# Delta-rule attention on one core: VectorE's value and key taps and substitution rows re-ordered, GpSimd's roots ahead of its weighting with two added waits, and the identity block loaded by DMA

## The chip, the cores and the metric

The kernel runs on 1 core of one Trainium2 chip. The metric is the device time of one execution in microseconds (us). Times of single instructions come from one profiled execution. Engines are named as the profile names them: PE (TensorE, with its weight loads as PEld), DVE (VectorE), ACT (ScalarE), POOL (GpSimd), SP (SyncE); SPq and ACTq are the DMA issues of SP and ScalarE.

## The reference, cut to what matters

Two layers follow each other, each with a residual and a layer norm: a gated delta-rule attention over 2 sequences of 2048 tokens (16 heads of 64), then a mixture of 64 experts. The change touches the attention alone.

```python
q = _causal_dwconv(x @ Wq.T, cq_w, cq_b)      # 4 taps in time, per channel; the same for k and v
k = _causal_dwconv(x @ Wk.T, ck_w, ck_b)
v = _causal_dwconv(x @ Wv.T, cv_w, cv_b)
g, beta = log_sigmoid(x @ Wg.T), sigmoid(x @ Wb.T)
k = k / clip(norm(k), 1e-12)
q = q * Kd ** (-0.5)
def step(S, inp):                              # over the 2048 tokens
    q_t, k_t, v_t, g_t, b_t = inp
    delta = k_t v_t^T - k_t (S k_t)^T
    S = exp(g_t) * S + b_t * delta
    o_t = S q_t
```

The kernel computes the recurrence in chunks of 64 tokens. Within a chunk that takes the inverse of a unit triangular 64x64 matrix; its 16x16 diagonal blocks are inverted by substitution, row by row, beginning from the identity, and the rest by products.

## The kernel before

**Work and slots.** The attention (`delta_phase`) has 64 macros: a macro m is one pair of heads over 256 tokens (4 chunks) of both sequences. All engines walk the same 71 slots t, each with a list of its own written out by hand in the code. In slot t the macro m = t is projected and convolved, the macro `before` = t-1 gets its lengths, decays and masked products, the macro `mi` = t-5 its inverse, and the state recurrence (the chain) of the macros 7 and more slots back advances by two chunks, `one` and `two_`. Two macros form a group of the substitution and of the chain, so that two slots, an odd and an even one, make a period. Nothing schedules: an engine runs its list in order, and semaphores order the engines.

**VectorE's list in a slot** (L658 to L701): last inverse product of the slot before (`horner`, L638), `residual(one)` (L646), three query taps (`conv`, L574), `gate` (L598), `update(one)` (L654), one key tap, `residual(two_)`, two key taps, `lengths` (L605), `inverse_lengths` (L609), `horner` after the product RX, `update(two_)`, two value taps (`conv_values`, L588), `horner` after RY1, `mask` (L617), which gives the masked products of `before`. In between lie the rows of the substitution (L628 and L631, two instructions a row, rows 0 to 14): 0 to 5 in the odd slot, 6 to 14 in the even one. Their shapes tell the rows: 128x15 is row 0 or row 14.

**The inverse's round trip.** When row 14 is done, ScalarE transposes the block (L757) and stores it (ACTq L764), SP stores it untransposed (SPq L307), SP then loads both in another layout (SPq L316, L321), and PE begins the product that needs them, `inverse_r` (L436, `delta_p_i<-delta_xd,noff`), in the odd slot ahead of `chain_state(two_)` (L470), whose result `residual(two_)` waits for. After these loads SP issues the loads of the next group's blocks, `kb` (SPq L299), without which its row 0 can't begin.

**PE's list** from there: `chain_state(two_)`, the value projection (L375), `chain_solve` (L495), RX (L436), `chain_update`, the query projection, RY1 (L436), `products` (L427), RY2 (L436, 64x16), which waits for VectorE's `horner` after RY1, and then the next slot.

**GpSimd's list in a slot** (L892 to L915): `decay_state(one)` (L888), `off_diagonal` (L858), `carry_in` (L844), `carry_out` (L851), in odd slots the copy of the identity into `xi` (L908), `decay_state(two_)`, `clip` (L863, after `lengths`), `factors` (L869, L870, after `inverse_lengths`), `weight` (L876), which `mask` waits for, and `roots` (L882).

## Time and profile before

| | |
|---|---|
| median of 3 runs | 1846.63 us (1846.21 to 1849.15) |
| profiled execution, its own time | 1854.48 us |
| its span in the profile | 1852.7 us |
| PE busy | 1576.1 us, 85% of the span |
| DVE busy | 1201.7 us, 65% |
| ACT busy | 890.0 us, 48% |
| POOL busy | 863.5 us, 47% |

The busy shares are means over the whole program. The attention's slots lie between some 75 and 1200 us of the span, and what follows is the mixture of experts, which the change doesn't touch. In the attention all four engines are busy in turn, so that a share says little; the times at which instructions of one period begin tell more. A row of the timeline reads: start, duration, engine, line, operation, tiles, count, and in brackets the idle time before it and what ended it. Lines are those of the kernel before.

### The profile page before, as it was taken

Reading aid. Unit: us, or ns where it says so; the run is one execution under the profiler, and the core shown is the slowest. Engines: PE = TensorE matmul, PEld = TensorE weight load, DVE = VectorE, ACT = ScalarE, POOL = GpSimd, SP = SyncE. Lnnn points to the kernel's source line nnn. Section 1 sums busy time; section 2 is a strip of 40 time slices with the busy share of each in tenths; the row PEclk is TensorE's granted clock in tenths of the full one; section 3 lists DMA queues with packets and bytes.
Section 4 is the critical chain, followed back from the end, with each engine's and each line's share of the span. In section 5 each row is a group of like instructions: output and inputs, shape, how many; then the busy total and the mean of one; then the engine's idle time right before and its main releaser. Section 6 shows DMA issues by size and latency. Waiting matters only on the chain. (4 is left out here: it accounts for less than half of the span.)

```text
span 1852.7 us, 73957 instructions
## 1 busy us (share of the span) xinstructions
PE 1576.1 (85%) x31244; PEld 1175.0 (63%) x31244; DVE 1201.7 (65%) x3061; ACT 890.0 (48%) x2282; POOL 863.5 (47%) x1070
## 2 busy tenths in 40 slices
PE   7478999999899999999999997667888985898990
PEld 6235666666666666666666665556777874787870
DVE  1388988888889889888888886234445553222224
ACT  1276767767767767667667664100011110133333
POOL 0034444443444444434444443116655665577775
PEclk9799999999999999999999998887889997999995
DMA  6235564565555655655656554274444420499757
GB/s 269 82 83 115 114 133 114 124 128 116 123 126 114 138 113 123 135 114 113 137 114 126 111 117 99 56 240 118 140 130 133 138 80 27 110 259 248 166 88 284
DMA packets 521402, 245.45 MB, mean 132 GB/s; under 512 B 423888, under 2 KB 485968, under 8 KB 520176
## 3 DMA queue, kind: packets, MB, share of 16 engines
q1 hardware_dynamic: 368976, 200.72, 41.2%
q10 hardware_dynamic: 133632, 20.98, 6.1%
q0 software_dynamic: 18464, 19.03, 5.8%
q8 instruction: 247, 4.05, 0.9%
q14 instruction: 83, 0.68, 0.1%
HBM read 169.29 MB, written 71.37 MB: 130 GB/s over the span
## 5 line engine op out<-in xcount | busy, mean ns | idle before, releaser
L375 PE MATMUL delta_p_j<-delta_xt,delta_w 128*128 128x512 f32 x768 | 387.7, 628 | 30.5 <-DMA delta_xt<-in_xt 17.5
L574 DVE SCALAR_TENSOR_TENSOR delta_kq<-delta_hist,cw,delta_kq 128x512 f32<-128x512 f32 x384 | 298.6, 778 | 30.7 <-ACT delta_kq L722 23.7
L1395 POOL DMA_INDIRECT slot_tokens<-mix_tokens,mix_slot x192 | 188.5, 982 | 115.5 <-DVE mix_slot L1266 59.8
L715 ACT ACTIVATE delta_hist<-delta_p_j 128x512 f32<-128x512 f32 x192 | 114.8, 598 | 240.6 <-PE delta_p_j L375 233.4
L375 PEld LDWEIGHTS delta_p_j<-delta_xt,delta_w 128*128 128x128 f32 x768 | 132.0, 192 | 146.3 <-issue 111.8
L888 POOL TENSOR_TENSOR delta_sd<-state,eg_end 128x256 f32<-128x256 f32 x128 | 104.4, 816 | 258.2 <-DVE state L654 258.2
L1074 PE MATMUL mix_p_y<-mix_wo,mix_ot 128*128 128x256 f32 x512 | 134.3, 407 | 33.3 <-issue 15.6
L863 POOL TENSOR_SCALAR delta_n<-delta_n 128x8 f32<-128x8 f32 x64 | 15.5, 242 | 287.3 <-DVE delta_n L605 287.3
L1165 PE MATMUL mix_p_h<-mix_wo,w 128*88 128x128 f32 x1024 | 126.2, 277 | 13.5 <-ACT mix_wo L1351 10.4
L588 DVE SCALAR_TENSOR_TENSOR delta_yv<-delta_hist,cw,delta_yv 128x512 f32<-128x512 f32 x128 | 132.1, 1032 | 8.2 <-ACT delta_yv L722 5.9
L1074 PEld LDWEIGHTS mix_p_y<-mix_wo,mix_ot 128*128 128x128 f32 x512 | 99.3, 202 | 58.3 <-issue 44.9
L778 ACT ACTIVATE delta_kpv<-delta_kpv,delta_root 128x64 f32<-128x64 f32 x512 | 135.3, 344 | 0.0
L1165 PEld LDWEIGHTS mix_p_h<-mix_wo,w 128*88 128x88 f32 x1024 | 115.8, 158 | 29.8 <-ACT mix_wo L1351 22.8
L882 POOL TENSOR_TENSOR delta_root<-delta_n,half_power 128x8 f32<-128x8 f32 x64 | 133.9, 2093 | 0.0
L436 PEld LDWEIGHTS delta_p_i<-delta_kkq,rt 64*32 64x32 f32 (+1 forms) x4096 | 67.3, 100 | 105.1 <-DVE delta_kkq L638 98.2
L495 PEld LDWEIGHTS delta_p_c<-delta_r,delta_kkq 64*64 64x64 f32 x2048 | 70.8, 136 | 93.6 <-issue 86.9
L772 ACT ACTIVATE delta_kpv<-delta_kpv,delta_fk 128x64 f32<-128x64 f32 x512 | 128.8, 343 | 0.1
L1301 DVE SCALAR_TENSOR_TENSOR mix_wo<-mix_wo,mix_p_h 88x256 f32<-88x256 f32 x64 | 26.7, 417 | 147.9 <-ACT mix_wo L1357 118.7
L1418 POOL DMA_INDIRECT acc<-mix_ot,mix_places x64 | 100.6, 1572 | 45.1 <-ACT mix_ot L1363 27.3
L436 PE MATMUL delta_p_i<-delta_kkq,rt 64*32 64x32 f32 (+1 forms) x4096 | 81.3, 184 | 44.4 <-DVE delta_kkq L638 43.6
L646 DVE TENSOR_TENSOR delta_r<-delta_kpv,delta_p_c 128x256 f32<-128x256 f32 x128 | 53.3, 416 | 87.4 <-PE delta_p_c L470 86.9
L631 DVE TENSOR_TENSOR delta_xi<-delta_xi,delta_outer 128x15 f32<-128x15 f32 (+7 forms) x480 | 99.0, 206 | 16.5
(148 smaller groups left out, 3607.5 us busy)
## 6 DMA issues: line engine op xcount, KB each, us to landing
delta_xd<-x_scratch SPq DMA_DIRECT2D x256, 128.0 KB
delta_w<-in_wqkv SPq DMA_DIRECT2D x64, 416.0 KB
w<-in_w SPq DMA_DIRECT2D x64, 352.0 KB
delta_eg<-eg_rows SPq DMA_DIRECT2D x128, 130.0 KB, 3.2
n_scratch<-delta_kkq ACTq DMA_DIRECT2D x128, 128.0 KB
ot<-delta_o SPq DMA_DIRECT2D x128, 128.0 KB
mix_ot<-ot SPq DMA_DIRECT2D x16, 1024.0 KB
w<-in_w SPq DMA_DIRECT2D x64, 176.0 KB
```

Of the source, the lines that this page charges most:

```text
L375: mm = pe.matmul(p_j[:, :], w[e][:, (ch * 3 + n) * 128:(ch * 3 + n) * 128 + 128], xt[m // 8 % 2][:, ch * 512:ch * 512 + 512], start=ch == ...
L436: mm = pe.matmul(view(p_i, g * C + first, (1, count), parts=(64 * sh, rows)), view(lhs, g * C, (1, rows), parts=half(sh)), view(rhs, at + ...
L574: ve.scalar_tensor_tensor(out, view(hist[e], i * 2 * 518 + tap, (259, 2), (1, 256)), cw[:, column:column + 1], out, ALU.mult, ALU.add).the ...
L588: ve.scalar_tensor_tensor(out, view(hist[e], 518 + tap, (259, 2), (1, 256)), cw[:, column:column + 1], out, ALU.mult, ALU.add).then_inc(co ...
L715: ac.activation(view(hist[e], n * 518 + 3, (259, 2), (1, 256)), p_j[:, :], ACT.Copy)
L772: ac.activation(kpv[:, at:at + C], kpv[:, at:at + C], ACT.Copy, scale=fk[:, g:g + 1]).then_inc(kp_out, 1)
L778: ac.activation(kpv[:, at:at + C], kpv[:, at:at + C], ACT.Copy, scale=root[:, g:g + 1]).then_inc(vp_out, 1)
L882: po.tensor_tensor(root[:, :], n2[:, :], view(s.half_power, 0, (0, 8)), ALU.pow).then_inc(small, 1)
L888: po.tensor_tensor(view(sd, 0, (128, 2), (C, 2), (1, C)), view(state, first_pair(group) * 128, (C, 2), (128, 2), (1, C)), view(s.eg_end, g ...
L1074: mm = pe.matmul(p_y[i % 2][:, 0:D], ot[i // 2 % 2][:, p * 256 + i % 2 * 128:p * 256 + i % 2 * 128 + 128], wo[:, p * D:p * D + D], start=p ...
L1165: mm = pe.matmul(p_h[e % 2][0:HALF, piece * 128:piece * 128 + 128], s.w13[:, at * 704 + ch * SI + piece * HALF:at * 704 + ch * SI + piece ...
L1395: po.indirect_dma_start(out=s.tok.ap(), out_offset=bass.IndirectOffsetOnAxis(ap=slot[i % 2][:, k:k + 1], axis=0), in_=tokens[:, i:i + 1], ...
```

## The change

Three things are changed, all in the attention.

- **VectorE.** The second value tap of a macro moves from the end of its slot to the next slot, ahead of the query taps. In odd slots all three key taps stand ahead of `residual(two_)`, and the value tap that is left stands behind `horner` after RY1. The odd slot takes rows 0 to 7 and the even slot rows 8 to 14; rows 4 to 7, and rows 13 and 14, stand behind `inverse_lengths` and `horner` after RX.
- **GpSimd.** Its slot begins with a wait for the first value tap of `before`; ahead of `decay_state(two_)` it waits for all key taps of m; `roots` stands ahead of `factors` and `weight`.
- **The identity** comes by a DMA on SP's queue (128 x 1 KB), issued ahead of the load of `kb`, in place of GpSimd's copy.

```diff
@@ load_blocks (SP) @@
                 sp.wait_ge(kk_out[group % 2], 64 * (group // 2 + 1))
+                if group >= 1:
+                    sp.wait_ge(x_out[(group - 1) % 2], 16 * ((group - 1) // 2 + 1))
+                    sp.wait_ge(xit_out, group)
+                sp.dma_start(xi[:, :], a["const"][:, C_EYE:C_EYE + SUB * SUB]).then_inc(xi_set, 16)
                 sp.dma_start(view(kb, 0, (SUB, SUB), (1, SUB)),
@@ VectorE @@
                 if is_macro(before):
+                    conv_values(before, 1)
                     conv(before, 1, tap_q, conv_q)
                     gate(before)
                 if even:
-                    substitute(subst_group, range(6, 9))
+                    substitute(subst_group, range(8, 9))
...
                 if is_macro(m):
-                    conv(m, 0, tap_k, conv_k, (2,))
+                    conv(m, 0, tap_k, conv_k, (2, 1, 0) if t % 2 else (2,))
                 if two_:
                     residual(*two_)
-                if is_macro(m):
+                if is_macro(m) and t % 2 == 0:
                     conv(m, 0, tap_k, conv_k, (1, 0))
...
                 if even:
-                    substitute(subst_group, range(11, SUB - 1))
+                    substitute(subst_group, range(11, 13))
                 if odd:
-                    substitute(subst_group, range(2, 6))
+                    substitute(subst_group, range(2, 4))
...
                     horner(mi, rx_done, 16, y1_out)
+                if even:
+                    substitute(subst_group, range(13, SUB - 1))
+                if odd:
+                    substitute(subst_group, range(4, 8))
                 if two_:
                     update(*two_)
-                if is_macro(m):
-                    conv_values(m)
+                if is_macro(m) and t % 2 == 0:
+                    conv_values(m, 2)
                 if is_macro(mi):
                     horner(mi, ry1_done, 32, y2_out)
+                if is_macro(m) and t % 2:
+                    conv_values(m, 2)
@@ GpSimd @@
             def roots(m):
+                po.wait_ge(clipped, m + 1)
...
+                if is_macro(before):
+                    po.wait_ge(conv_v, 2 * before + 1)
                 if one:
                     decay_state(*one)
...
-                if t % 2 and 0 <= (t - 3) // 2 < NG:
...
-                    po.tensor_copy(xi[:, :], const[:, C_EYE:C_EYE + SUB * SUB]).then_inc(xi_set, 1)
+                if is_macro(m):
+                    po.wait_ge(conv_k, 3 * m + 3)
                 if two_:
                     decay_state(*two_)
                 if is_macro(before):
                     clip(before)
+                    roots(before)
                     factors(before)
                     weight(before)
-                    roots(before)
```

VectorE in an odd slot, from `lengths` on, before (rows 2 to 5, `inverse_lengths`, `horner`, `update(two_)`, value taps):

```order
L605 TENSOR_REDUCE delta_n2<-delta_sq 128x8
L628 TENSOR_TENSOR delta_outer<-delta_xi,delta_kb 128x39
L631 TENSOR_TENSOR delta_xi<-delta_xi,delta_outer 128x3x13
L628 TENSOR_TENSOR delta_outer<-delta_xi,delta_kb 128x48
L631 TENSOR_TENSOR delta_xi<-delta_xi,delta_outer 128x4x12
L628 TENSOR_TENSOR delta_outer<-delta_xi,delta_kb 128x55
L631 TENSOR_TENSOR delta_xi<-delta_xi,delta_outer 128x5x11
L628 TENSOR_TENSOR delta_outer<-delta_xi,delta_kb 128x60
L631 TENSOR_TENSOR delta_xi<-delta_xi,delta_outer 128x6x10
L609 RECIPROCAL delta_rn<-delta_n2 128x8
L638 TENSOR_TENSOR delta_kkq<-delta_xd0,delta_p_i 128x8x48
L654 TENSOR_TENSOR state<-delta_sd,delta_p_c 128x2x2x64
```

and after, from `inverse_lengths` to the value tap:

```order
L612 RECIPROCAL delta_rn<-delta_n2 128x8
L641 TENSOR_TENSOR delta_kkq<-delta_xd0,delta_p_i 128x8x48
L631 TENSOR_TENSOR delta_outer<-delta_xi,delta_kb 128x55
L634 TENSOR_TENSOR delta_xi<-delta_xi,delta_outer 128x5x11
L631 TENSOR_TENSOR delta_outer<-delta_xi,delta_kb 128x60
L634 TENSOR_TENSOR delta_xi<-delta_xi,delta_outer 128x6x10
L631 TENSOR_TENSOR delta_outer<-delta_xi,delta_kb 128x63
L634 TENSOR_TENSOR delta_xi<-delta_xi,delta_outer 128x7x9
L631 TENSOR_TENSOR delta_outer<-delta_xi,delta_kb 128x64
L634 TENSOR_TENSOR delta_xi<-delta_xi,delta_outer 128x8x8
L657 TENSOR_TENSOR state<-delta_sd,delta_p_c 128x2x2x64
L641 TENSOR_TENSOR delta_kkq<-delta_xd0,delta_p_i 128x8x32
```

Two rows left the stretch ahead of `inverse_lengths`, and four stand now between the two `horner` instructions.

VectorE at the end of the substitution in an even slot, before:

```order
L628 TENSOR_TENSOR delta_outer<-delta_xi,delta_kb 128x39
L631 TENSOR_TENSOR delta_xi<-delta_xi,delta_outer 128x13x3
L628 TENSOR_TENSOR delta_outer<-delta_xi,delta_kb 128x28
L631 TENSOR_TENSOR delta_xi<-delta_xi,delta_outer 128x14x2
L628 TENSOR_TENSOR delta_outer<-delta_xi,delta_kb 128x15
L631 TENSOR_TENSOR delta_xi<-delta_xi,delta_outer 128x15
L609 RECIPROCAL delta_rn<-delta_n2 128x8
L638 TENSOR_TENSOR delta_kkq<-delta_xd1,delta_p_i 128x8x48
```

and after:

```order
L631 TENSOR_TENSOR delta_outer<-delta_xi,delta_kb 128x39
L634 TENSOR_TENSOR delta_xi<-delta_xi,delta_outer 128x13x3
L612 RECIPROCAL delta_rn<-delta_n2 128x8
L641 TENSOR_TENSOR delta_kkq<-delta_xd1,delta_p_i 128x8x48
L631 TENSOR_TENSOR delta_outer<-delta_xi,delta_kb 128x28
L634 TENSOR_TENSOR delta_xi<-delta_xi,delta_outer 128x14x2
L631 TENSOR_TENSOR delta_outer<-delta_xi,delta_kb 128x15
L634 TENSOR_TENSOR delta_xi<-delta_xi,delta_outer 128x15
```

The reciprocal and one `horner` now stand ahead of rows 13 and 14.

GpSimd over one slot after the change, with its waits:

```order
L899 TENSOR_TENSOR delta_sd<-state,eg_end 128x256 [waits d_s_out,d_conv_k]
L873 TENSOR_SCALAR delta_n<-delta_n 128x8 [waits d_norms]
L893 TENSOR_TENSOR delta_root<-delta_n,half_power 128x8 [waits d_vp_out,d_clipped]
L879 TENSOR_TENSOR delta_bp<-beta,delta_rn 128x8 [waits d_kp_out,d_recip]
L880 TENSOR_TENSOR delta_fk<-kd,delta_rn 128x8
L886 TENSOR_TENSOR ex<-ex,delta_bp 128x8x64 [waits d_factors,d_exped]
L899 TENSOR_TENSOR delta_sd<-state,eg_end 128x256 [waits d_s_out,d_conv_v]
L868 TENSOR_TENSOR noff<-delta_kkq,const 128x8x48 [waits d_pe_r,d_masked]
```

The roots (L893) stood behind the weighting (L886) before, and the two `decay_state` (L899) waited for `d_s_out` alone.

## Rows read from the trace of the kernel before

**Rows 1.** Waits, 200 to 1000 us: who waited for what, total, times, longest.

```profile
DVE delta_r L646 <- PE delta_p_c L470: 58.1, 47, 3.3
```

**Rows 2.** The masks of line 617, 200 to 1000 us: durations, first and last start.

```profile
L617 DVE TENSOR_TENSOR delta_kkq<-delta_p_xy,ex x47: 1215/1217/1226, 212.7 to 989.3; 128x1024 f32<-128x1024 f32 x47
```

**Rows 3.** Timeline of DVE, row 14 of one group, then the odd slot.

```profile
597.40 0.18 DVE L631 TENSOR_TENSOR delta_xi<-delta_xi,delta_outer 128x15 f32<-128x15 f32 x1
...
606.60 0.75 DVE L574 SCALAR_TENSOR_TENSOR delta_kq<-delta_hist,cw,delta_kq 128x512 f32<-128x512 f32 x1
609.90 0.42 DVE L646 TENSOR_TENSOR delta_r<-delta_kpv,delta_p_c 128x256 f32<-128x256 f32 x1 [2.56 <-PE delta_p_c L470]
...
611.69 0.17 DVE L628 TENSOR_TENSOR delta_outer<-delta_xi,delta_kb 128x15 f32<-128x15 f32 x1
...
612.42 0.68 DVE L605 TENSOR_REDUCE delta_n<-delta_sq 128x8 f32<-128x512 f32 x1
```

**Rows 4.** Timeline of DVE, the even slot behind it, to the next row 14.

```profile
626.28 0.42 DVE L646 TENSOR_TENSOR delta_r<-delta_kpv,delta_p_c 128x256 f32<-128x256 f32 x1 [0.15 <-PE delta_p_c L470]
...
628.06 0.21 DVE L628 TENSOR_TENSOR delta_outer<-delta_xi,delta_kb 128x60 f32<-128x60 f32 x1
...
631.15 0.18 DVE L631 TENSOR_TENSOR delta_xi<-delta_xi,delta_outer 128x15 f32<-128x15 f32 x1
631.24 0.19 DVE L609 RECIPROCAL delta_rn<-delta_n 128x8 f32<-128x8 f32 x1
631.35 0.50 DVE L638 TENSOR_TENSOR delta_kkq<-delta_xd,delta_p_i 128x384 f32<-128x384 f32 x1
631.77 0.41 DVE L654 TENSOR_TENSOR state<-delta_sd,delta_p_c 128x256 f32<-128x256 f32 x1
```

**Rows 5.** Timeline of PE in the same two slots.

```profile
608.45 1.08 PE L436 MATMUL delta_p_i<-delta_xd,noff 64*64 64x48 f32 x30 [0.77 <-DMA delta_xd<-x_scratch]
...
618.24 0.57 PE L436 MATMUL delta_p_i<-delta_kkq,rt 64*16 64x16 f32 x32 [0.68 <-DVE delta_kkq L638]
...
625.97 0.23 PE L470 MATMUL delta_p_c<-state,delta_kqg 64*64 64x64 f32 x2
```

**Rows 6.** Timeline of another period: two rows 14, and what lies between.

```profile
698.47 0.18 DVE L631 TENSOR_TENSOR delta_xi<-delta_xi,delta_outer 128x15 f32<-128x15 f32 x1
...
711.77 0.17 DVE L628 TENSOR_TENSOR delta_outer<-delta_xi,delta_kb 128x15 f32<-128x15 f32 x1
...
731.23 0.18 DVE L631 TENSOR_TENSOR delta_xi<-delta_xi,delta_outer 128x15 f32<-128x15 f32 x1
```

**Rows 7.** Timeline of PE in that period.

```profile
708.57 1.03 PE L436 MATMUL delta_p_i<-delta_xd,noff 64*64 64x48 f32 x30
```

**Rows 8.** Timeline of POOL and DVE, instructions of both that overlap in time.

```profile
598.35 1.36 DVE L588 SCALAR_TENSOR_TENSOR delta_yv<-delta_hist,cw,delta_yv 128x512 f32<-128x512 f32 x1
...
598.12 1.04 POOL L876 TENSOR_TENSOR ex<-ex,delta_bp 128x512 f32<-128x512 f32 x1
599.12 2.12 POOL L882 TENSOR_TENSOR delta_root<-delta_n,half_power 128x8 f32<-128x8 f32 x1
601.21 0.62 POOL L888 TENSOR_TENSOR delta_sd<-state,eg_end 128x256 f32<-128x256 f32 x1
...
606.76 1.06 POOL L888 TENSOR_TENSOR delta_sd<-state,eg_end 128x256 f32<-128x256 f32 x1 [2.38 <-DVE state L654]
```

**Rows 9.** Key and query taps, 600 to 1000 us: durations in ns, least, median, most.

```profile
L574 DVE SCALAR_TENSOR_TENSOR delta_kq<-delta_hist,cw,delta_kq x144: 742/752/934, 602.4 to 998.6; 128x512 f32<-128x512 f32 x144
```

**Rows 10.** Timeline, one period in which row 0 waited for `kb`.

```profile
496.45 0.18 DVE L631 TENSOR_TENSOR delta_xi<-delta_xi,delta_outer 128x15 f32<-128x15 f32 x1
...
510.19 0.17 DVE L628 TENSOR_TENSOR delta_outer<-delta_xi,delta_kb 128x15 f32<-128x15 f32 x1 [0.35 <-DMA delta_kb<-n_scratch]
```

**Rows 11.** SP's issues of the `kb` load, 400 to 1000 us: durations in ns.

```profile
L299 SPq DMA_DIRECT2D delta_kb<-n_scratch x18: 376/562/1786, 403.7 to 977.4; - x18
```

**Rows 12.** GpSimd beside the substitution rows, timeline of POOL.

```profile
613.19 0.24 POOL L863 TENSOR_SCALAR delta_n<-delta_n 128x8 f32<-128x8 f32 x1 [5.37 <-DVE delta_n L605]
```

25 lines of the change are left out of this document (10 added, 15 removed).

## The prediction

> **What bounds the kernel now.** I read first the waits of the attention, then one period of two slots in the timelines of VectorE, PE and GpSimd. The shares of busy time decide nothing here: in the attention VectorE and PE are both busy nearly all the time. The waits name the one long wait of VectorE: `residual(two_)` for PE's `chain_state`, 58.1 us in 47 times [rows 1]. The masks give the period: 46 slots between 212.7 and 989.3 us, 16.88 us each, so 33.77 us for an odd and an even slot [rows 2].
>
> The timelines show why that wait is there. I count from E, the end of row 14 of a group (597.40 + 0.18 = 597.58) [rows 3]. From E the inverse goes by ScalarE, two DMAs and back, and PE begins `inverse_r` at 608.45, after a wait of 0.77 for the load [rows 5]: 10.87 us after E. PE then runs its list to the even slot's `chain_state(two_)`, which ends at 625.97 + 0.23 = 626.20, 17.75 us later; of these 0.68 are a wait for VectorE's `horner` ahead of RY2 [rows 5]. VectorE's even `residual(two_)` starts at 626.28, and the next E is 631.15 + 0.18 = 631.33, 5.05 us later [rows 4]. So the period of 33.75 us is a loop: 10.87 (round trip) + 17.75 (PE) + 0.08 + 5.05 (VectorE). Another period, of 32.76 us (698.65 to 731.41), has no such DMA wait: there PE begins at 708.57, 9.92 us after E [rows 6, 7]. What matters is what the change does to this loop, and the idle 2.56 us of VectorE in the odd slot [rows 3] are not on it.
>
> **The key taps moved into the idle time.** In the odd slot two key taps, 2 x 0.75 = 1.5 us [rows 3], leave the stretch behind `residual(two_)` and run while VectorE waits. They cost nothing there: the cover is the 2.56 us [rows 3], of which 1.1 are left. But row 0 then waits for its block: before, it starts 13.12 us after E without a wait [rows 6], in another period at 510.19, 13.56 us after E (496.63), released by the `kb` load [rows 10]. So `kb` lands about 13 us after E, and the taps' gain ends there.
>
> **The identity by DMA.** GpSimd loses a copy that lay beside nothing critical. On SP's queue one issue now stands ahead of `kb`'s. No row shows it; the `kb` issue takes 0.38, 0.56 or 1.79 us (least, median, most) [rows 11], so `kb` lands from 0.4 to 1.8 us later, and I take 0.5, near the median. The two new waits on SP (`x_out`, `xit_out`) were passed already by the loads before them. Row 0 is then at 13.2 us after E, taken a little over the 13.12 [rows 6], with 13.6 as what rows 10 would give.
>
> **The second value tap.** It cost 1.36 us in place of 0.75 for the first of the two, beside the weighting, which had begun 0.23 us earlier (598.12 against 598.35) [rows 8]; a key tap alone takes 0.75 [rows 3, 9]. The loss of 0.61 goes. The later tap is free of it anyway and only moves to the next slot. VectorE's work from row 0 (611.69) to the even `residual(two_)`, 14.44 us without the 0.15 of idle [rows 3, 4], shrinks by 0.61, and by 0.18 for a query tap that took 0.934 in place of 0.752 [rows 9]: 13.65. So VectorE reaches the even residual 13.2 + 13.65 = 26.85 us after E. PE gets there, without its wait of 0.68, at 9.92 + 17.07 + 0.08 = 27.07 in the one period and at 10.87 + 17.15 = 28.02 in the other. PE stays the later: VectorE's relief ahead of this point is worth no more than the 0.68.
>
> **Rows 13 and 14 behind `horner`.** The reciprocal (631.24 to 631.35) and the product (631.35 to 631.77) now stand ahead of row 14 [rows 4]: the last piece of the loop grows by 0.11 + 0.42 = 0.53, to 5.58. Rows 6 and 7 move from the even slot to the odd one within the PE piece, and don't enter. Without anything else the loop is 10.87 + 17.07 + 0.08 + 5.58 = 33.60 (before 33.75), and 9.92 + 17.07 + 0.08 + 5.58 = 32.65 (before 32.76). PE may start earlier in the second, since no wait shows when its load landed; VectorE's own work bounds that: 13.2 + 13.65 + 5.58 = 32.43. **That part is worth 0.11 to 0.33 us a period**, far less than the five edits suggest.
>
> **Where GpSimd's work falls now.** Two collisions are new. The rows of a substitution, like the value tap, read two tiles of SBUF, and in the trace no long GpSimd instruction lies beside them; only `clip` does, without harm [rows 12]. The masks, with an input in PSUM, keep 1.215 to 1.226 us [rows 2] beside roots and `decay_state`.
> - Collision A, odd slot. Weighting begins, counted from row 0, after `lengths` (0.73 + 0.68), `clip` (0.09 + 0.24 [rows 3, 12]), the roots (2.12 [rows 8]) and the two factors (0.2 each, an estimate from `clip`): 4.3 us. A row's instruction takes 0.22 with its gap ((631.33 - 628.06 - 0.68 for `lengths`) / 12 [rows 4]). Rows 4 to 7, eight of them, run from the same start after 0.73 + 0.68, 0.9 for rows 2 and 3, 0.11 and 0.42, so from 2.8 to 4.6, later where RX is late. So their end lies in the weighting. The value tap was held until 0.84 us after the weighting's start (0.23 + 0.61) [rows 8]; that is the most, zero the least. PE's lead over VectorE covers 0.2 (27.07 - 26.85) in the quick period, so 0.6 of it counts; in the slow one the cover is 1.2 (28.02 - 26.85), less 0.5, my estimate for VectorE's wait for the late RX, so 0.1 counts.
> - Collision B, even slot. `decay_state(two_)` now waits for the key taps and so starts with row 9 (628.06 before [rows 4]), where before it began 0.16 us behind a key tap and was itself the one held back, 1.06 in place of 0.62 [rows 8]. It has 0.62 us; taking off the 0.20 that the weighting did not hold (1.04 - 0.84) gives 0.42. It lies in the last piece of the loop, without cover. Bounds: 0 and 0.62.
>
> The Trainium skill (SBUF — State Buffer, section "Who interferes with whom") says that VectorE with two SBUF inputs and a GpSimd instruction that reads SBUF exclude each other for the whole instruction, and whoever is first holds the other up. The held tap and the held `decay_state` [rows 8] agree. By that rule A and B would be 1.04 and 0.62 at most; by the rows 0.84 and 0.42. It speaks against this placement, since it makes no exception for short instructions.
>
> In the even slot the roots end about when row 14 does, and the weighting meets the value tap only if VectorE comes second; the mask waits for PE's products there, so I cost it at nothing.
>
> **The sum.** Slow period: -0.15 + 0.10 + 0.42 = +0.37. Quick period: -0.11 + 0.60 + 0.42 = +0.91. The mean period, 33.77, is nearly the slow one; I give it two thirds: 0.25 + 0.30 = +0.55 us. Slots 7 to 63 have all of the work: 28.5 periods, +15.7 us. Start and end of the attention, without chain or without taps, I put at nothing. The profiled execution took 1854.48 us and would take 1870.2; the median is 7.85 lower, 1846.63, so **1862.3 us**.
>
> **The rivals.**
> - *GpSimd holds no row up* (the instructions are too short to be caught, as with `clip`). Then only the loop's 0.11 to 0.33 remain: 3 to 9 us faster, 1838 to 1843, middle 1841. For it: no row of the trace shows a substitution instruction being held. Against it: the tap. This is the side opposite to my forecast; it decides from A + B below 0.15.
> - *`kb` becomes the bound.* If the two DMAs cost 1.2 us in place of 0.5, row 0 is at 14.3 and VectorE at the residual 14.3 + 13.65 + 0.84 = 28.8, later than PE in both; with 0.08, 5.58 and 0.42 the period is 34.9, +1.1: 31 us slower, 1878.
> - *Nothing comes of it*: the little gain of the loop and a little of B cancel, or VectorE is first in each meeting and GpSimd alone is held. 1847.
> - *The round trip shortens*, because stores and loads meet other traffic: then PE alone bounds, 33.75 - 0.77 - 2 x 0.68 = 31.6 a period, 61 us faster, 1785. Against it: nothing in the change moves the four transfers of the trip.
>
> **How the numbers follow.** Forecast 0.45, no hold-up 0.20, nothing 0.16, `kb` 0.14, short trip 0.05. The range leaves out the short trip and the upper part of the `kb` case: 1839 to 1879. Some 0.2% (3.7 us) is about what a measurement of this kernel can tell from no change. Faster by more: most of the second case and the last, 0.22. Within: 0.20. Slower: the forecast and `kb`, 0.58.
>
> **What would show it.** In the changed profile: row 9's instructions (or the gap before them) longer by 0.4 in even slots, and rows 6 or 7 by up to 0.8 in odd ones; VectorE's value taps at 0.75; PE's wait ahead of RY2 gone; the wait of `residual(two_)` in odd slots down to about 1 us; the time from E to `inverse_r` unchanged, and 5.6 to 6.0 from the even residual to E. Row 0 released by the `kb` load in most periods. I am wrong if the rows keep their lengths beside GpSimd, if the trip from E changes by more than 0.5, or if `kb` comes over 14 us after E.

## The result, and the profile after

The changed kernel takes 1867.69 us (median of 4 runs, 1865.54 to 1879.11), the kernel before 1846.42 us beside it (4 runs, 1845.01 to 1849.15). The ratio is 1.0126, 95% interval 1.0083 to 1.0169: about 21 us slower, where 15.7 were forecast. A second measurement of the same change, r1 below, gave 1.0119.

The stage behind the attention is the same in all of these kernels, and yet it differs by up to some 17 us from profile to profile on chips of like times (641 to 658 us from the last update of the state on). So I measure the attention by the masks, from the first of the 64 to the last. Source of the mask's line in the changed kernel, the whole span, then 200 to 1000 us:

```profile
L620 DVE TENSOR_TENSOR delta_kkq<-delta_p_xy,ex x64: 1211/1224/1226, 89.4 to 1160.2; 128x1024 f32<-128x1024 f32 x64
```

```profile
L620 DVE TENSOR_TENSOR delta_kkq<-delta_p_xy,ex x47: 1216/1224/1226, 199.0 to 989.9; 128x1024 f32<-128x1024 f32 x47
```

And the same of the kernel before, the whole span:

```profile
L617 DVE TENSOR_TENSOR delta_kkq<-delta_p_xy,ex x64: 1208/1217/1226, 89.2 to 1140.5; 128x1024 f32<-128x1024 f32 x64
```

The masks span 1070.8 us after and 1051.3 before: +19.5. The period is 790.9 / 46 x 2 = 34.39 us, against 33.77 [rows 2]: +0.62, where +0.55 was forecast. The masks leave out the last slots, in which only inverse and chain run on. Source of the update of the state, before and after:

```profile
L654 DVE TENSOR_TENSOR state<-delta_sd,delta_p_c x128: 410/412/422, 169.0 to 1201.4; 128x256 f32<-128x256 f32 x128
L657 DVE TENSOR_TENSOR state<-delta_sd,delta_p_c x128: 408/414/422, 169.0 to 1223.0; 128x256 f32<-128x256 f32 x128
```

By the last update the attention ends 21.6 us later, which is the 21 us of the timed runs.

**What became of the waits.** Waits of the changed kernel, 200 to 1000 us (who waited for what: total, times, longest):

```profile
POOL delta_sd L899 <- DVE delta_kq L578: 339.5, 47, 8.6
...
DVE delta_r L649 <- PE delta_p_c L474: 34.7, 30, 3.0
DVE delta_outer L631 <- DMA delta_kb<-n_scratch: 33.9, 23, 2.9
...
PE delta_p_i L440 <- DMA delta_xd<-x_scratch: 20.7, 17, 2.0
...
PE delta_p_i L440 <- DVE delta_kkq L641: 14.5, 15, 1.7
```

`residual` waits less for PE (58.1 us in [rows 1]), but row 0 now waits for `kb` in nearly every group (0.6 us in 2 before), and PE for the load of `xd` in 17 (6.3 us in 7 times before). The first row is GpSimd's new wait for the key taps.

**Who is held up.** Groups of VectorE by shape in the changed kernel, 200 to 1000 us (busy us, mean ns, idle before):

```profile
L591 DVE SCALAR_TENSOR_TENSOR delta_yv<-delta_hist,cw,delta_yv 128x512 f32<-128x512 f32 x93 | 69.8, 751 | 0.0
...
L634 DVE TENSOR_TENSOR delta_xi<-delta_xi,delta_outer 128x63 f32<-128x63 f32 x46 | 21.1, 458 | 1.6
L634 DVE TENSOR_TENSOR delta_xi<-delta_xi,delta_outer 128x60 f32<-128x60 f32 x46 | 19.3, 420 | 1.6
...
L631 DVE TENSOR_TENSOR delta_outer<-delta_xi,delta_kb 128x60 f32<-128x60 f32 x46 | 13.8, 300 | 0.8
L631 DVE TENSOR_TENSOR delta_outer<-delta_xi,delta_kb 128x63 f32<-128x63 f32 x46 | 13.8, 300 | 0.8
```

And the answering groups of the kernel before:

```profile
L588 DVE SCALAR_TENSOR_TENSOR delta_yv<-delta_hist,cw,delta_yv 128x512 f32<-128x512 f32 x94 | 98.9, 1052 | 1.7
L631 DVE TENSOR_TENSOR delta_xi<-delta_xi,delta_outer 128x63 f32<-128x63 f32 x48 | 10.8, 224 | 1.6
L628 DVE TENSOR_TENSOR delta_outer<-delta_xi,delta_kb 128x63 f32<-128x63 f32 x48 | 10.6, 221 | 0.8
L631 DVE TENSOR_TENSOR delta_xi<-delta_xi,delta_outer 128x60 f32<-128x60 f32 x48 | 10.6, 221 | 1.6
L628 DVE TENSOR_TENSOR delta_outer<-delta_xi,delta_kb 128x60 f32<-128x60 f32 x48 | 10.4, 217 | 0.8
```

A period has four value taps. They lost 4 x (1.052 - 0.751) = 1.20 us a period to GpSimd before, and lose nothing now. The twelve key and query taps lost 12 x (0.776 - 0.749) = 0.32 before, and nothing now. Each shape of a row occurs twice a period: the four shown lose 2 x (0.234 + 0.199 + 0.083 + 0.079) = 1.19 us now, and lost nothing before: 0.40 of it in row 9 (collision B), 0.79 in rows 5 and 6 (collision A). So the time lost to GpSimd is not larger than it was; it moved from the taps, where PE was later anyway, to the substitution.

Timeline of VectorE in the changed kernel, end of an even slot and the odd slot behind it (start, duration, idle before and releaser in brackets):

```profile
601.81 0.42 DVE L649 TENSOR_TENSOR delta_r<-delta_kpv,delta_p_c 128x256 f32<-128x256 f32 x1
...
603.59 0.21 DVE L631 TENSOR_TENSOR delta_outer<-delta_xi,delta_kb 128x60 f32<-128x60 f32 x1
603.84 0.62 DVE L634 TENSOR_TENSOR delta_xi<-delta_xi,delta_outer 128x60 f32<-128x60 f32 x1
...
607.48 0.18 DVE L634 TENSOR_TENSOR delta_xi<-delta_xi,delta_outer 128x15 f32<-128x15 f32 x1
...
621.02 0.42 DVE L649 TENSOR_TENSOR delta_r<-delta_kpv,delta_p_c 128x256 f32<-128x256 f32 x1 [2.73 <-PE delta_p_c L474]
622.87 0.17 DVE L631 TENSOR_TENSOR delta_outer<-delta_xi,delta_kb 128x15 f32<-128x15 f32 x1 [1.43 <-DMA delta_kb<-n_scratch]
```

Timeline of GpSimd beside it:

```profile
603.76 0.62 POOL L899 TENSOR_TENSOR delta_sd<-state,eg_end 128x256 f32<-128x256 f32 x1 [6.98 <-DVE delta_kq L578]
```

`decay_state(two_)` starts with row 9's second instruction and holds it, 0.62 us in place of 0.22. From the even residual to E (607.66) it is 5.85 us, against 5.05 before [rows 4]. Row 0 starts 15.21 us after E in this group, which is one of the late ones: the mean of 23 groups is 13.58 (table below).

Another odd slot shows both ends of the collision with the weighting. Timeline of VectorE, then of GpSimd, then of PE:

```profile
318.61 0.27 DVE L631 TENSOR_TENSOR delta_outer<-delta_xi,delta_kb 128x63 f32<-128x63 f32 x1
318.92 0.99 DVE L634 TENSOR_TENSOR delta_xi<-delta_xi,delta_outer 128x63 f32<-128x63 f32 x1
...
320.67 0.41 DVE L641 TENSOR_TENSOR delta_kkq<-delta_xd,delta_p_i 128x256 f32<-128x256 f32 x1
```

```profile
318.78 1.04 POOL L886 TENSOR_TENSOR ex<-ex,delta_bp 128x512 f32<-128x512 f32 x1
```

```profile
321.14 0.57 PE L440 MATMUL delta_p_i<-delta_kkq,rt 64*16 64x16 f32 x32 [1.67 <-DVE delta_kkq L641]
```

Row 6 takes 0.99 in place of 0.22; the four rows stand ahead of the `horner` after RY1 (320.67), and PE waits 1.67 us for it ahead of RY2. The wait of 0.68 in [rows 5] is rarer (28.3 us in 42 times before, 14.5 in 15 now) but, where it comes, up to 1.7 us long.

### The profile page after: what moved, and what is told of

Same layout as the page of the kernel before. It is cut to its first block and busy times, and to the rows that moved or that the text cites. A ratio compares the mean times of both kernels' runs of the same rounds, so it can differ in the third digit from the quotient of the medians.

```text
span 1864.3 us, 74142 instructions
## 1 busy us (share of the span) xinstructions
PE 1583.8 (85%) x31244; PEld 1182.7 (63%) x31244; DVE 1185.6 (64%) x3061; ACT 891.3 (48%) x2282; POOL 789.9 (42%) x1038
## 5 line engine op out<-in xcount | busy, mean ns | idle before, releaser
L379 PE MATMUL delta_p_j<-delta_xt,delta_w 128*128 128x512 f32 x768 | 392.6, 635 | 47.1 <-ACT delta_kq L732 19.1
L578 DVE SCALAR_TENSOR_TENSOR delta_kq<-delta_hist,cw,delta_kq 128x512 f32<-128x512 f32 x384 | 287.6, 749 | 32.5 <-ACT delta_kq L732 24.4
L899 POOL TENSOR_TENSOR delta_sd<-state,eg_end 128x256 f32<-128x256 f32 x128 | 79.3, 620 | 529.9 <-DVE delta_kq L578 411.6
L1083 PE MATMUL mix_p_y<-mix_wo,mix_ot 128*128 128x256 f32 x512 | 126.3, 392 | 28.2 <-DMA mix_wo<-in_wo 15.2
L631 DVE TENSOR_TENSOR delta_outer<-delta_xi,delta_kb 128x15 f32<-128x15 f32 (+7 forms) x480 | 106.7, 222 | 58.8 <-DMA delta_kb<-n_scratch 50.0
L634 DVE TENSOR_TENSOR delta_xi<-delta_xi,delta_outer 128x15 f32<-128x15 f32 (+7 forms) x480 | 125.8, 262 | 16.5
L893 POOL TENSOR_TENSOR delta_root<-delta_n,half_power 128x8 f32<-128x8 f32 x64 | 108.5, 1695 | 5.4
L440 PE MATMUL delta_p_i<-delta_xd,noff 64*64 64x48 f32 x2048 | 77.9, 227 | 36.1 <-DMA delta_xd<-x_scratch 34.2
```

Of the source, the lines that this page charges most:

```text
L379: mm = pe.matmul(p_j[:, :], w[e][:, (ch * 3 + n) * 128:(ch * 3 + n) * 128 + 128], xt[m // 8 % 2][:, ch * 512:ch * 512 + 512], start=ch == ...
L440: mm = pe.matmul(view(p_i, g * C + first, (1, count), parts=(64 * sh, rows)), view(lhs, g * C, (1, rows), parts=half(sh)), view(rhs, at + ...
L578: ve.scalar_tensor_tensor(out, view(hist[e], i * 2 * 518 + tap, (259, 2), (1, 256)), cw[:, column:column + 1], out, ALU.mult, ALU.add).the ...
L634: ve.tensor_tensor(view(xi, row + 1, (SUB, i), (1, left)), view(xi, row + 1, (SUB, i), (1, left)), view(outer, 0, (left, i), (1, left)), A ...
L893: po.tensor_tensor(root[:, :], n2[:, :], view(s.half_power, 0, (0, 8)), ALU.pow).then_inc(small, 1)
L1083: mm = pe.matmul(p_y[i % 2][:, 0:D], ot[i // 2 % 2][:, p * 256 + i % 2 * 128:p * 256 + i % 2 * 128 + 128], wo[:, p * D:p * D + D], start=p ...
```

## The experiments

"Masks" is the time from the first to the last mask in a kernel's own profile: 1051.3 for the kernel before, 1070.8 for the changed one. A time in brackets behind a ratio is the median; the kernel before took 1852.46 us beside e1 to e4, 1847.71 beside e5 to e8 and 1845.10 beside r1, e9 and e10. The interval of a ratio is 9 to 32 us wide, that of a difference of two ratios wider, and a masks time is that of one profile. The two measures agree in sign on what every edit does to the changed kernel, and differ by up to 9 us in size. So the price of a single edit is known to some us at best.

The same by pieces: means in us over the 23 groups (24 in e6) whose E lies between 200 and 1000 us, read from the timelines. "To the residual" is to the even `residual(two_)`.

| | before | changed | r1 | e1 | e2 | e3 | e6 |
|---|---|---|---|---|---|---|---|
| period, E to E | 33.76 | 34.36 | 34.32 | 34.05 | 33.82 | 33.98 | 32.84 |
| E to `inverse_r` | 10.40 | 10.14 | 9.83 | 10.01 | 10.04 | 10.12 | 10.06 |
| `inverse_r` to the residual | 18.28 | 18.33 | 18.62 | 18.54 | 18.31 | 17.98 | 17.69 |
| residual to E, the last piece | 5.08 | 5.88 | 5.88 | 5.49 | 5.47 | 5.88 | 5.08 |
| E to row 0 | 13.73 | 13.58 | 13.57 | 13.70 | 13.49 | 12.81 | 12.69 |
| groups with row 0 over 14 us | 9 | 9 | 8 | 10 | 8 | 1 | 2 |
| groups in which the residual waits for PE | 22 | 12 | 11 | 11 | 11 | 13 | 17 |

The last row matters most: before, PE was the later engine at the residual in nearly every group; in the changed kernel VectorE is, in about half of them.

**r1.** The changed kernel, measured again.

> The changed kernel once more, on the chip of the other two kernels of this group. The first comparison had 4 runs and gave a ratio of 1.0083 to 1.0169. Expected 1.010 to 1.014. If it is below 1.008, part of what the experiments were said to give back was scatter between chips; from the first mask to the last its profile should again show 1065 to 1075 us against 1051 before.

Measured: 1.0119, 1.0072 to 1.0166 (1866.92 us against 1845.10); masks 1070.2 us, `kb` waited for 40.6 us in 22 times. The loss stands, and two profiles of one kernel agree within 0.6 us in the masks, though not within that in the wait for `kb` (33.9 and 40.6).

**e1.** `decay_state(two_)` no longer waits for the key taps.

```diff
                     carry_out(before)
-                if is_macro(m):
-                    po.wait_ge(conv_k, 3 * m + 3)
                 if two_:
```

> The changed kernel without GpSimd's wait for the key taps ahead of decay_state(two_). Theory (the last piece of the loop, from the even residual to row 14, is lengthened by row 9, held 0.40 us by decay_state): GpSimd is the one held up again, row 9 is 0.22 us, 28.5 x 0.40 = 11 us off the 1867.7, about 1856. Rival (the loads of the blocks set the period): row 0 comes no earlier, the time stays within 4 us of 1867. Third possibility: decay_state then catches another key tap in odd slots, which lies in idle time and costs nothing.

Measured: 1.0018, 0.9995 to 1.0042 (1858.53 us); masks 1059.6, 11.2 less. Group of VectorE in e1, 200 to 1000 us:

```profile
L634 DVE TENSOR_TENSOR delta_xi<-delta_xi,delta_outer 128x60 f32<-128x60 f32 x47 | 11.2, 237 | 1.6
```

From 420 to 237 ns: row 9 is free, and the last piece is 0.39 us shorter. 11.2 / 28.5 = 0.39 us a period too, against the 0.42 of the prediction. Collision B is shown in kind, and its size by the profile; the ratio fell by more, 0.0108 or 20 us, where 11 were expected, and its interval leaves room for both. The third possibility came true beside it: `decay_state` now holds one tap of the odd slot (0.25 us in 23 groups).

**e2.** Rows 13 and 14 back ahead of `inverse_lengths` and `horner`.

```diff
                 if even:
-                    substitute(subst_group, range(11, 13))
+                    substitute(subst_group, range(11, SUB - 1))
...
-                if even:
-                    substitute(subst_group, range(13, SUB - 1))
```

> The changed kernel with rows 13 and 14 back ahead of the reciprocal and the product after RX in even slots. Theory (loop): row 14 ends 0.53 us earlier in each period, 15 us off, about 1853. Rival (PE sets the period, since its RY1 now gets the product 0.8 us later): PE shows a new wait for that product and the time stays near 1867.

Measured: 1.0045, 1.0018 to 1.0072 (1862.26 us); masks 1053.3, 17.5 less, or 0.61 a period where the step had 0.53. Of these the last piece gives 0.41 (5.88 to 5.47), and nothing shows cover for it; the rest came elsewhere. The sign of the rival is there, but small: PE waits 24.8 us for `horner` ahead of RY2, against 14.5. Group of VectorE in e2:

```profile
L591 DVE SCALAR_TENSOR_TENSOR delta_yv<-delta_hist,cw,delta_yv 128x512 f32<-128x512 f32 x94 | 88.9, 946 | 0.0
```

The even value tap is held again, by 0.81 us in 23 groups, 4 x 0.195 = 0.78 a period, and the kernel is faster all the same. A tap held there costs little.

**e3.** The identity by GpSimd's copy again, behind `carry_out` in odd slots; no DMA ahead of `kb`.

```diff
-                sp.dma_start(xi[:, :], a["const"][:, C_EYE:C_EYE + SUB * SUB]).then_inc(xi_set, 16)
...
-                        ve.wait_ge(xi_set, 16 * (group + 1))
+                        ve.wait_ge(xi_set, group + 1)
...
+                    po.tensor_copy(xi[:, :], const[:, C_EYE:C_EYE + SUB * SUB]).then_inc(xi_set, 1)
```

> The changed kernel with the identity copied by GpSimd as in the kernel before. Row 0 was released by the load of the blocks in 23 of 23 periods of the changed kernel. Theory A (the identity's DMA ahead of it costs the 0.55 us between the two issues): row 0 comes 0.5 us earlier, 14 us off, about 1854. Theory B (the blocks' load is late by itself, in about half of the periods by 2.5 us, whatever is ahead of it): row 0 keeps its two values, near 12.6 and 15.2 us after row 14, and the time stays within 4 us of 1867.

Measured: 1.0064, 1.0033 to 1.0095 (1864.77 us); masks 1057.7, 13.1 less, 0.46 a period. Waits of e3, 200 to 1000 us:

```profile
DVE delta_outer L627 <- DMA delta_kb<-n_scratch: 15.7, 19, 2.0
...
PE delta_p_i L436 <- DVE delta_kkq L637: 2.3, 4, 1.0
```

The wait for `kb` halves (33.9 before the edit), and row 0 comes 0.77 us earlier on average, with 1 group over 14 us in place of 9. Across the kernels it is the same: with VectorE's new order the wait is 8.8 to 22.4 us in the four with GpSimd's copy (e3, e6, e7, e10), 33.9 to 40.6 in those with the DMA ahead of `kb`. PE's wait ahead of RY2 goes with it (14.5 us in 15 times before the edit), which fits a VectorE that is late at the `horner` because it was late at row 0. So the DMA of the identity, which I had put on record as hidden, is on the path. The timed ratio agrees (0.62% less), but its interval overlaps the changed kernel's. The edit also gives GpSimd a copy, so that the price of the DMA alone may be a little more.

**e4.** The load of `kb` ahead of the identity's, both by DMA.

```diff
                 sp.wait_ge(kk_out[group % 2], 64 * (group // 2 + 1))
+                sp.dma_start(view(kb, 0, (SUB, SUB), (1, SUB)),
+                             bass.AP(s.n_scratch[group % 2], 0, [[LANE, 128], [C, SUB], [1, SUB]])).then_inc(kb_in, 16)
                 if group >= 1:
...
                 sp.dma_start(xi[:, :], a["const"][:, C_EYE:C_EYE + SUB * SUB]).then_inc(xi_set, 16)
-                sp.dma_start(view(kb, 0, (SUB, SUB), (1, SUB)),
-                             bass.AP(s.n_scratch[group % 2], 0, [[LANE, 128], [C, SUB], [1, SUB]])).then_inc(kb_in, 16)
```

> The changed kernel with SP issuing the blocks' load ahead of the identity's DMA. Theory A: the blocks come 0.5 us earlier, but the identity is now the last of the two; if its 128 large packets land quickly, row 0 gains up to 0.5 us a period, 1854 to 1867. Theory B (late by itself): the same as the changed kernel, within 4 us.

Measured: 1.0146, 1.0082 to 1.0211 (1879.81 us, 4 runs); masks 1077.3, 6.5 more, where 0 to 14 less was expected: a miss. Group of VectorE in e4, 200 to 1000 us:

```profile
L631 DVE TENSOR_TENSOR delta_outer<-delta_xi,delta_kb 128x15 f32<-128x15 f32 x46 | 8.1, 176 | 43.7 <-DMA delta_xi<-in_const 42.9
```

Row 0 then waits for the identity, 42.9 us, against 33.9 and 40.6 for `kb` in the two profiles of the changed kernel. So to put `kb` first gains nothing. That it loses is seen in the profile alone, since the timed intervals overlap; and that the extra transfer costs wherever it stands is argued from e3 and e4, not shown by itself.

**e5.** In odd slots the weighting ahead of the roots, and the update of the state ahead of rows 4 to 7.

```diff
-                if odd:
-                    substitute(subst_group, range(4, 8))
                 if two_:
                     update(*two_)
+                if odd:
+                    substitute(subst_group, range(4, 8))
...
-                    roots(before)
+                    if t % 2 == 0:
+                        roots(before)
                     factors(before)
                     weight(before)
+                    if t % 2:
+                        roots(before)
```

> The changed kernel; in odd slots GpSimd's weighting stands ahead of the roots again and VectorE's update(two_) ahead of rows 4 to 7, so that the weighting runs beside instructions that read PSUM. Theory (collision A costs 0.1 to 0.6 us a period, since PE's lead covers a part of its 0.78): rows 4 to 7 all at 0.22, 3 to 10 us off the changed kernel, ratio to the kernel before 1.007 to 1.011. Rival (A is wholly on the path): 22 us off, ratio about 1.001. Rival (A is wholly covered): nothing.

Measured: 1.0112, 1.0074 to 1.0150 (1868.40 us against 1847.71); masks 1061.5, 9.3 less. Group of VectorE in e5, 200 to 1000 us:

```profile
L634 DVE TENSOR_TENSOR delta_xi<-delta_xi,delta_outer 128x63 f32<-128x63 f32 x47 | 10.5, 224 | 1.6
```

Row 6 is free, from 458 to 224 ns. But rows 4 to 7 are not all at 0.22, as the theory had it. Group of the first instruction of rows 4 and 10 in e5, and the timeline of one odd slot, VectorE and GpSimd:

```profile
L631 DVE TENSOR_TENSOR delta_outer<-delta_xi,delta_kb 128x55 f32<-128x55 f32 x47 | 20.1, 427 | 0.8
```

```profile
316.05 0.88 DVE L631 TENSOR_TENSOR delta_outer<-delta_xi,delta_kb 128x55 f32<-128x55 f32 x1
```

```profile
315.81 1.04 POOL L886 TENSOR_TENSOR ex<-ex,delta_bp 128x512 f32<-128x512 f32 x1
```

The weighting (1.04 us) outlasts the update that it was to run beside, and holds row 4 instead, in 19 of 23 groups (214 ns before the edit). Collision A fell from 0.79 to 2 x 0.213 = 0.43 us a period and is not gone. The masks give 0.33 us a period for the 0.36 taken away, the mean period of the 23 groups 0.24 (34.12 us); the timed ratio can't be told from the 1.0126 of the changed kernel. So collision A is shown in kind, its price rests on profiles, and no run has the kernel without it.

**e9.** e1 and e5 together.

> The changed kernel without both collisions (no wait for the key taps; in odd slots weighting ahead of the roots and update(two_) ahead of rows 4 to 7), everything else as changed: identity by DMA, rows 13 and 14 last. Theory (A and B are together 0.4 + some 0.3 us a period and add): some 20 us below the changed kernel, ratio 1.000 to 1.003, first to last mask some 1050 us. Rival (once one is gone the loads of the blocks hold row 0, and the other brings nothing): 1.003 to 1.007, some 1060 us.

Measured: 1.0045, 1.0019 to 1.0070 (1850.06 us against 1845.10); masks 1050.5, 20.3 less. Singly 11.2 and 9.3: they add up. The ratio lies above the 1.000 to 1.003 expected and within the rival's 1.003 to 1.007; the masks and the last update of the state (1203.8 us, 20 less) are the theory's. The timed ratio is 0.8% less than the changed kernel's, the intervals just apart. Row 9 is free, but row 4 is still held. Group of VectorE in e9:

```profile
L631 DVE TENSOR_TENSOR delta_outer<-delta_xi,delta_kb 128x55 f32<-128x55 f32 x48 | 23.2, 484 | 0.8
```

So 0.71 us a period is what the two edits take away: all of B, and of A's 0.79 us all but 2 x 0.27 = 0.54. PE's wait ahead of RY2 is what it was. Waits of e9:

```profile
PE delta_p_i L440 <- DVE delta_kkq L641: 15.1, 16, 1.5
```

**e6.** e1, e2, e3 and e5 together.

> All together: no wait for the key taps, rows 13 and 14 ahead of the product, identity by GpSimd, odd weighting ahead of the roots and update(two_) ahead of rows 4 to 7; of the change there remain the moved value tap, the key taps in the idle time, the seven rows in odd slots and the wait for the value tap. Theory (the parts add up: 11 + 15 + 12 + 5 us): some 43 us below the changed kernel, ratio to the kernel before 0.985 to 0.992. Rival (PE and the round trip bound it before that): the loop 10.87 + 17.07 + 0.08 + 5.05 is 33.1 us, 0.7 a period below before, 19 us, ratio 0.990. Rival (another wait takes the place of each): ratio 0.998 or more.

Measured: **0.9897, 0.9863 to 0.9930** (1828.29 us against 1847.71), 1.0% faster than the kernel before and 2.3% faster than the changed one; masks 1022.7, 48.1 less, where the four apart sum to 51.1. Waits of e6, 200 to 1000 us:

```profile
DVE delta_r L645 <- PE delta_p_c L470: 20.4, 30, 2.5
...
DVE delta_outer L627 <- DMA delta_kb<-n_scratch: 10.1, 19, 1.9
```

What is left of GpSimd's holds lies mainly on the value taps again (0.961 us on average, 4 x 0.21 = 0.84 a period), where it costs little; row 4 keeps 2 x 0.144 = 0.29. The first rival's 0.990 fits the ratio as well as the theory does, so that the ratio doesn't decide between them; the period, 0.92 us below that of the kernel before where the rival had 0.7, speaks for the theory.

**e10.** e6 without GpSimd's wait for the first value tap.

```diff
-                if is_macro(before):
-                    po.wait_ge(conv_v, 2 * before + 1)
```

> The kernel e6_all without GpSimd's wait for the first value tap at the start of its slot. Theory (the wait only keeps decay_state(one) from holding a value tap that is off the loop, or is itself later than GpSimd would be anyway): within 0.3% of e6_all, ratio to before 0.987 to 0.993. Rival (the wait is what makes e6_all good, since off_diagonal and decay_state then meet the masks alone): taps are held again by 0.4 to 0.6 us and the ratio rises to 0.995 or more.

Measured: 0.9948, 0.9919 to 0.9977 (1834.29 us against 1845.10); masks 1033.4, 10.7 more than e6. Group of VectorE in e10:

```profile
L630 DVE TENSOR_TENSOR delta_xi<-delta_xi,delta_outer 128x64 f32<-128x64 f32 x24 | 17.0, 708 | 0.8
```

Row 7, 225 ns before, is held, by `decay_state(one)` and `off_diagonal`, and so is the value tap behind it in 14 groups (0.44 us). The ratio lies above the 0.987 to 0.993 expected and just under the rival's 0.995, and the two intervals overlap a little. So the new wait is worth having by the profile: it keeps GpSimd behind a tap that has begun.

**e7 and e8.** The two lists apart: e7 is the kernel before with VectorE's new order alone, e8 with GpSimd's new order and waits alone.

> VectorE's list of the change alone, with GpSimd's list, waits and identity of the kernel before. Theory: the weighting now begins right behind the reciprocal, so that in even slots rows 13 and 14 are held by up to 0.84 us, on the last piece of the loop, and in odd ones rows 4 to 7 by 0.3 to 0.8; row 9 is free. Ratio to the kernel before 1.010 to 1.020. Rival (the list is good by itself and only GpSimd's new order and waits cost): ratio 1.000 or less, in which case the collisions would not be the cause.

> GpSimd's order and waits of the change alone (roots ahead, the waits for the value tap and for the key taps), with VectorE's list and the identity copy of the kernel before. Theory: row 9 is held 0.40 us in even slots, on the last piece of the loop; the value taps are held by the weighting as before; decay_state(one), which starts with the second value tap, holds that one too. Ratio 1.005 to 1.012. Rival (harmless without VectorE's list): 1.000.

Measured, e7: 1.0080, 1.0042 to 1.0118 (1865.03 us): below the 1.010 to 1.020 expected, which its interval still reaches. Its masks are 1053.9, only 2.6 more than those of the kernel before; from the last mask to the last update it takes 8.5 us more (69.8 against 61.3), so that here the masks alone would mislead. Row 13 is held in even slots as expected. Group of VectorE in e7:

```profile
L630 DVE TENSOR_TENSOR delta_xi<-delta_xi,delta_outer 128x28 f32<-128x28 f32 x47 | 26.7, 569 | 1.6
```

That is 2 x 0.381 = 0.76 us a period (188 ns before). Row 0 waits 22.4 us for `kb` in e7, though no DMA stands ahead of it: part of the wait comes with VectorE's order, which brings it to row 0 earlier.

e8: 1.0376, 1.0291 to 1.0462 (1917.43 us, 4 runs), a miss by a factor of three. Groups of VectorE in e8, 200 to 1000 us:

```profile
L588 DVE SCALAR_TENSOR_TENSOR delta_yv<-delta_hist,cw,delta_yv 128x512 f32<-128x512 f32 x90 | 120.3, 1337 | 1.6
...
L631 DVE TENSOR_TENSOR delta_xi<-delta_xi,delta_outer 128x60 f32<-128x60 f32 x45 | 18.6, 413 | 1.5
...
L631 DVE TENSOR_TENSOR delta_xi<-delta_xi,delta_outer 128x15 f32<-128x15 f32 x45 | 17.7, 394 | 1.5
```

Timeline of VectorE in e8, behind an even `update`:

```profile
618.72 2.80 DVE L588 SCALAR_TENSOR_TENSOR delta_yv<-delta_hist,cw,delta_yv 128x512 f32<-128x512 f32 x2
```

In the old order of VectorE the key taps end right ahead of row 0 in odd slots, so `decay_state` is released into row 0 there (394 ns) as into row 9 (413); and both value taps stand ahead of the `horner` that RY2 needs and are both held, 2.80 us for 1.5 of work. Together the two lists cost less than GpSimd's alone; in the changed kernel the odd key taps end in VectorE's idle time, which fits, but no run parts this from the rest. A wait on the other engine's progress is good or bad only with that engine's list.

**e11.** Behind some of the longer idle times of PE the clock granted to TensorE fell. Windows of PE in the changed kernel behind its wait of 1.85 us for `xd`, up to which the granted clock was 1.00 (length, PE busy and its instructions, granted clock, DMA share, GB/s):

```profile
618.70:619.70 1.00, 1.00 (x22) 0.59 0.93 233
619.70:620.70 1.00, 1.00 (x35) 0.50 1.44 166
620.70:621.70 1.00, 1.00 (x24) 0.50 0.18 19
621.70:622.70 1.00, 1.00 (x2) 0.71 0.05 3
```

0.50 is the lower level, 1.2 GHz of 2.4. The wait of 1.67 us above is followed by such a stretch too. In windows of one microsecond from 90 to 1160 us, the share missing from full clock adds up to 8.5 us before and 17.1 after (r1: 20.5); from 200 to 1000 us to 0.0, 8.5 and 13.7. In e11 PE transposes chunks 2 and 3 of the values twice in odd slots, so that it stands idle for less.

```diff
-                    turn_values(before, (2, 3))
+                    turn_values(before, (2, 3), 2 if t % 2 else 1)
```

> The changed kernel, but in odd slots PE transposes chunks 2 and 3 of the values twice, with the same result, right ahead of inverse_r. In the profile of the changed kernel one such pass takes 0.70 us (616.13 to 616.83), and PE then stood idle 1.85 us for the load of xd before inverse_r at 618.68, after which the granted clock of TensorE was 0.59, 0.50, 0.50, 0.71 in the next four microseconds. Between 90 and 1160 us the clock lost there adds up to 17.1 us in windows of one microsecond (8.5 in the kernel before). Theory (the clock falls because PE stood idle so long): with the idle time cut by 0.7, the stretches at half clock directly behind the load wait, four of them between 160 and 1100 us, go or all but go, and the loss falls to 10 to 13 us; those behind the wait ahead of RY2 stay. The extra pass itself costs nothing where PE waits for the load anyway (17 of 23 periods in 200 to 1000 us) and up to 0.7 us in the others. So the time falls by up to 7 us or rises by up to 5. Rival (the clock falls at random moments, whatever PE does): the loss stays at 16 to 20 us and stretches at half clock still begin behind the load wait.

Measured: 1.0113, 1.0077 to 1.0148 (1785.48 us against 1762.29; on this chip both kernels are 82 to 84 us shorter, in e11 nearly all of it behind the attention: 560.8 us from the last update on, against 640.9); masks 1068.8; clock missing 3.4 us, all of it before 130 us. So the stretches at half clock behind the load wait are gone, as expected, but those behind the wait ahead of RY2 are gone too, which was not, and one of these waits was 1.61 us long. The chip is another one, so that it is not shown that the added work did it. And the time hardly moved: 2.0 us less in the masks, with up to 28 passes of 0.70 us in them. What the clock costs of the 21 us is not isolated. Three profiles speak against much: with 3.4 (e11), 17.1 (changed) and 20.5 us (r1) missing, the last update of the state ends at 1223.8, 1223.4 and 1224.4 us. Still, e2 has no such stretch from 200 to 1000 us, and part of its 17.5 us may be that.

## Why the prediction was right, and where it was off

The way and nearly the size came out, but in part by luck. The forecast of +0.55 us was +0.95 in the last piece (0.53 and 0.42) and -0.40 in the rest of the loop. By the table it was +0.80 and -0.20, so that two errors of like size cancelled.

- **The bound.** E to `inverse_r` is 11.02 us in the group shown (10.87 before); on average it is 10.14, or 9.83 in r1, against 10.40. The loop through E, the round trip, PE's list and the last piece was read rightly for the kernel before: the residual waits for PE in 22 of 23 groups. What the change takes from or adds to the last piece counts (e1, e2: 0.39 and 0.41 there, for 0.42 and 0.53). Ahead of it "PE stays the later" held in 12 of 23 groups only.
- **Key taps into the idle time, free.** As said; what was left of the idle, "down to about 1 us", came out at 34.7 us in 30 waits, 1.2 each, but with 2.73 in a group whose `xd` came late.
- **Identity by DMA.** This is the step that failed. It put `kb` 0.5 later and let the lead of PE (26.85 against 27.07) hide it. The load's issue stands 0.55 us later in the row below, but row 0 moved by 0.77 (12.81 in e3, 13.58 with the DMA), and in 11 of 23 groups no lead of PE was left to hide it. Removing the DMA gives 13.1 us of the masks back (e3). The starting point was wrong too: 13.12 was the time from E to row 0 of quick groups, and the mean before was 13.73. In the group of [rows 3] itself row 0 started at 611.69, 14.11 after E. So "over 14 us after E" was no sign of anything: 9 of 23 groups are over it in either kernel; what is new is that all 23 wait for `kb`. The rival in which `kb` is the bound came true in some groups only. Timeline of SP in the changed kernel:

```profile
617.91 0.50 SPq L302 DMA_DIRECT2D delta_xi<-in_const  x1
618.46 0.43 SPq L303 DMA_DIRECT2D delta_kb<-n_scratch  x1
```

- **Value tap.** 0.751 us, as said. What frees it is the place of the weighting (e2, where it is held again), not the wait for the first value tap; by e10 that wait is worth 10.7 us of the masks in e6.
- **PE's wait ahead of RY2.** Rarer, but not gone: 14.5 us in 15 times. I had not reckoned with VectorE late at row 0. Without the identity's DMA the wait is 2.3 us in 4 (e3) and 0.7 in 1 (e6). Collision A stands ahead of that `horner` too, but has the smaller part in it: with A in part gone it is 8.9 in 12 (e5) and 15.1 in 16 (e9).
- **Rows 13 and 14.** 0.53 in the step, 0.41 in the last piece and 0.61 by the masks (e2). The reciprocal costs nothing there: from the second instruction of row 12 to row 13 it was 0.23 us before (630.26 to 630.49), and it is 0.65 now (606.18 to 606.83), 0.42 more, which is the `horner` alone.
- **Collision A.** 0.77 on the row (0.99 for 0.22) in one slot, up to 0.84 forecast, and 0.79 a period held on average. The step let PE's lead cover most of it and priced it at 0.27, the mean of the two cases. e5 takes 0.36 of the 0.79 away and gains 0.33 by the masks, 0.24 by the mean period and 0.09 by the timed ratio. Scaled up by 0.79 / 0.36 that is an estimate of 0.2 to 0.7 for the whole: how much was covered stays open.
- **Collision B.** 0.42 forecast, 0.40 on the row, 0.39 a period by e1. The Trainium skill (SBUF — State Buffer, "Who interferes with whom") has a VectorE instruction with two SBUF inputs and a GpSimd instruction that reads SBUF exclude each other for the whole instruction. The rows agree that one of them waits and that a short row is no exception. In size they stay below it: the row of 603.84 began 0.08 us behind a `decay_state` of 0.62 us, ended 0.08 behind it, and lost 0.40.
- **The sum.** The four harmful parts (rows, B, A, identity) were 0.53 + 0.42 + 0.27 + 0 = 1.22 us a period, and what the four edits gave back by the masks was 0.61 + 0.39 + 0.33 + 0.46 = 1.79, or 1.69 together (48.1 / 28.5), with a part of A still there. The rest of the change was to bring 0.68 (33.75 less 33.60 - 0.53), and e6 shows 1.00 (its masks are 28.6 us below those of the kernel before). Harm and gain were both too small, by at least 0.5 and 0.3, so the net, +0.55 against +0.68 by the masks, came out nearer than its terms, and that is luck. The largest miss is the identity, 0 for 0.46.
- **The rivals.** "GpSimd holds no row up" is refuted by the row of 0.62; "nothing" by the interval; the round trip did not shorten as that rival had it: E to `inverse_r` is 0.3 us less on average (0.6 in r1), and PE's wait for `xd` grew from 6.3 to 20.7 us, since PE now comes to it earlier.

## What to carry to other kernels

No order tried here was without holds between VectorE and GpSimd: they summed to 0.8 us a period in e5 and e9, some 1.5 before, 1.2 after the change and 2.0 in e2. What they cost went by where they lay, not by their sum: e2 has 0.8 more of them than the changed kernel and still gained all that the move of its rows was to give. So when an instruction is moved, find out where its hold lands, and let it land beside work that another engine hides (here: a value tap, an idle stretch), not in the last piece of the loop. A wait that makes an engine off the path start later is such a move as well. And a small DMA put ahead of a load that someone waits for was on the path here; look at how much slack the load's landing has, over many groups and not in one.

## What the runs showed of the hardware

- The power of 128 x 8 elements on GpSimd took 2.11 us on average before, where it began beside a value tap, and 1.70 now, beside rows, though it reads next to nothing. Its two copies of 18 elements, `carry_in` and `carry_out`, took 0.62 and 0.20 us before, and 0.20 and 0.43 now. Groups of GpSimd in the changed kernel, 200 to 1000 us:

```profile
L893 POOL TENSOR_TENSOR delta_root<-delta_n,half_power 128x8 f32<-128x8 f32 x46 | 78.1, 1698 | 3.9
L886 POOL TENSOR_TENSOR ex<-ex,delta_bp 128x512 f32<-128x512 f32 x46 | 60.0, 1305 | 0.0
```

- Whoever comes second waits: in odd slots the weighting takes 1.04 and the row 0.99, in even ones the tap has begun and the weighting takes 1.56 (mean 1.305).
- The granted clock fell to 0.50 behind some idle times of PE, with 1.7 us missing in each of the five stretches of the changed kernel from 200 to 1000 us. The length of the wait alone does not decide it: it fell behind one of 1.63 us, and not behind another of 1.67; in r1 it fell behind one of 1.20.
- `kb` lands late in some groups and not in others, with the same issues ahead of it on SP's queue. The cause stays open.
